# Unread TensorE products between the steps of a causal attention, and layer weights loaded later

## What is computed

```python
qkv = einsum('bsi,oi->bso', x, w_qkv) + b_qkv       # x: 2 x 1024 x 128
q, k = rope(q), rope(k)
scores = einsum('bhqd,bhkd->bhqk', q, k) / sqrt(8)
scores = where(causal, scores, lowest)
ex = exp(scores - max(scores))
attn = ex / (sum(ex) + 1e-8)
out = einsum('bhqk,bhkd->bhqd', attn, v) @ w_out.T + b_out
```

## Time and profile before

| | us |
|---|---|
| median of three runs | 2311.33 (2304.25 to 2318.38) |
| the profiled execution | 2307.12 |
| its span, first to last instruction | 2305.3 |
| TensorE busy | 2014.6 (87%) |
| VectorE busy | 1809.4 (78%) |
| ScalarE busy | 1665.7 (72%) |
| GpSimd busy | 1267.5 (55%) |
| mean granted TensorE clock | 0.941 |

### The profile page before, as it was taken

One profiled execution on the slowest core, in us unless ns is written; L12 is line 12 of the kernel. 1 busy time (PEld: TensorE's weight loads), 2 busy tenths in 40 slices (PEclk: granted clock), 3 DMA queues, 4 the chain that ended last, 5 costly groups with the idle time before them and its releaser, 6 DMA issues. The chain is left out here.

```text
span 2305.3 us, 55541 instructions
## 1 busy us (share of the span) xinstructions
PE 2014.6 (87%) x20349; PEld 1353.3 (59%) x20349; DVE 1809.4 (78%) x3609; ACT 1665.7 (72%) x3163; POOL 1267.5 (55%) x1132
## 2 busy tenths in 40 slices
PE   5788888579999999999999999999999999984283
PEld 3233332346766776776767677677767776673152
DVE  4666660699999999999999999999999999834623
ACT  2265555378888888888898888888888888864123
POOL 4400000477777677767777776776677677711052
PEclk8799997699999999999999999999999999996587
DMA  6321100211111121111211111101211111100511
GB/s 160 97 58 26 23 2 2 66 36 38 29 38 29 30 86 29 38 29 38 77 38 29 39 57 49 38 29 38 77 38 29 33 35 32 35 20 26 186 35 66
DMA packets 70562, 107.36 MB, mean 47 GB/s; under 512 B 20887, under 2 KB 47774, under 8 KB 68734
## 3 DMA queue, kind: packets, MB, share of 16 engines
q1 hardware_dynamic: 68262, 100.87, 15.2%
q0 software_dynamic: 1280, 2.62, 0.4%
q10 hardware_dynamic: 752, 0.33, 0.1%
HBM read 41.60 MB, written 12.26 MB: 23 GB/s over the span
## 5 line engine op out<-in xcount | busy, mean ns | idle before, releaser
L1446 POOL TENSOR_TENSOR qk<-rot_cos,rot_sin 128x512 f32<-128x512 f32 x256 | 323.2, 1274 | 160.3 <-DVE rot_sin L1247 160.3
L1245 DVE TENSOR_TENSOR rot_cos<-pA,layer_tab 128x512 f32<-128x512 f32 x384 | 262.8, 684 | 65.6 <-ACT sq L1086 58.7
L1456 POOL TENSOR_TENSOR qk<-qk,rnorm 128x512 f32<-128x512 f32 x256 | 262.9, 1043 | 88.0 <-DVE rnorm L1280 88.0
L382 ACT ACTIVATE probs_by_key<-pT 128x512 f32<-128x512 f32 (+3 forms) x384 | 176.9, 489 | 155.2 <-PE pT L298 119.8
L1086 ACT ACTIVATE sq<-pA 128x512 f32<-128x512 f32 x384 | 228.4, 595 | 55.9 <-PE pA L873 46.1
L439 DVE TENSOR_REDUCE minus_max<-pS 128x1 f32<-128x1024 f32 (+7 forms) x256 | 184.3, 753 | 106.4 <-PE pS L270 105.8
L1257 DVE TENSOR_REDUCE sumsq<-sq 128x8 f32<-128x512 f32 x384 | 253.4, 670 | 14.8 <-ACT sq L1086 14.6
L1247 DVE TENSOR_TENSOR rot_sin<-pA,layer_tab 128x512 f32<-128x512 f32 x384 | 260.8, 679 | 0.0
L1146 ACT ACTIVATE probsT<-pD 64x512 f32<-64x512 f32 x384 | 226.4, 589 | 43.8 <-PE pD L914 40.3
L1463 POOL TENSOR_TENSOR probs<-probs,row_inverse 128x1024 f32<-128x1024 f32 x96 | 182.7, 1904 | 104.9 <-DVE row_inverse L1316 104.9
L1106 ACT ACTIVATE qT<-pC 64x512 f32<-64x512 f32 x384 | 225.9, 588 | 7.3 <-PE pC L888 0.5
(11 more groups left out here) (313 smaller groups left out, 4619.4 us busy)
## 6 DMA issues: line engine op xcount, KB each, us to landing
v_shifted<-v SPq DMA_DIRECT2D x96, 384.0 KB, 3.5
v_shifted<-v SPq DMA_DIRECT2D x95, 128.0 KB, 3.4
q_stack<-stacked SPq DMA_DIRECT2D x24, 192.0 KB
k_stack<-stacked SPq DMA_DIRECT2D x24, 192.0 KB
W_ahead<-in_Wqkv_dram SPq DMA_DIRECT2D x12, 384.0 KB
layer_weights<-in_Wqkv_dram SPq DMA_DIRECT2D x12, 384.0 KB
stacked<-part SPq DMA_DIRECT2D x32, 128.0 KB, 2.4
tokens_in<-tokens SPq DMA_DIRECT2D x2, 1024.0 KB
```

The lines of the kernel that those rows point to most:

```text
L1245: dve.tensor_tensor(t1[c % 2][:, :].rearrange("p (h g d) -> p h g d", g=2, d=32), a, tabl[s % 2][:, j].unsqueeze(1).broadcast_to([P, 8, 2, ...
L1446: pool.tensor_tensor(qk(s, c), t1[c % 2][:, :], t2[c % 2][:, :], ALU.add).then_inc(added[c], 1)
L1456: pool.tensor_tensor(v, v, rn[p % 2][:, o:o + 8].unsqueeze(2).broadcast_to([P, 8, DH]), ALU.mult).then_inc(scaled[c], 1)
```

## The change

A helper `filler(out, n)` issues `n` bf16 products of the identity with the 256 columns of `cm` into a PSUM region that nobody reads. They stand: 60 before the first row block; 2 behind each of the row blocks 14 to 42; 2 behind the blocks at u = 1 and 3 of every later group and 3 behind `turn_maxima` there; 1 behind each of the last 66 pieces. The first two kinds write `OT[1]` and bring two waits for kept jobs; the others write the second bank of the `S` tensor whose first bank holds a narrow block or the maxima. And the load of the first window layer's weights and of the two tables moves in SP's queue from ahead of the loop over groups to behind the stacks of group 7 (g = 4).

```diff
@@ -203,15 +203,16 @@
                 load_stacks(g)
             sp.wait_ge(w_turned, 2)
             sp.dma_start(wr[:, 0, :], w["a_b_out"].rearrange("(a n) -> a n", a=1).broadcast_to([P, D])).then_inc(bo_in, 16)
-            load_layer(sp, w, env["W0"], 0, env["w0_loaded"])
-            sp.dma_start(env["xpos"][:], w["xpos"]).then_inc(env["const_loaded"], 16)
-            sp.dma_start(env["mask"][:], w["mask"]).then_inc(env["const_loaded"], 16)
             for g in range(GROUPS):
                 load_maxima(g)
                 if g < 2:
                     late_stores(2 + g)
                 if g >= 1 and g - 1 + SLOTS_G < GROUPS:
                     load_stacks(g - 1 + SLOTS_G)
+                if g == 4:
+                    load_layer(sp, w, env["W0"], 0, env["w0_loaded"])
+                    sp.dma_start(env["xpos"][:], w["xpos"]).then_inc(env["const_loaded"], 16)
+                    sp.dma_start(env["mask"][:], w["mask"]).then_inc(env["const_loaded"], 16)
 
         @block.tensor
         def _(pe):
@@ -257,6 +258,14 @@
             pe.wait_ge(mask_in, 16)
             pe.wait_ge(ident_cast, 1)
 
+            def filler(out, n):
+
+                for _ in range(n):
+                    pe.matmul(out, identb[:, :], cm[:, :, :], start=True, stop=True, skip_group_check=True)
+
+            def half_of(at):
+                return S[at % 2][:, 512:512 + 2 * P]
+
             def row_block(g, u):
                 h, qt = u // TB, TURNS[u % TB]
                 at, r = rows_at(g, u), g % SLOTS_G
@@ -315,18 +324,29 @@
             done = 0
             for j in range(EARLY_JOBS):
                 job(j)
+            pe.wait_ge(job_kept, 4)
+            filler(OT[1][:, 0:2 * P], 60)
             for it in range(GROUPS + 2):
                 if it == GROUPS:
                     turn_maxima(GROUPS - 1)
                 for u in range(NS):
                     if it < GROUPS:
                         row_block(it, u)
+                        if 14 <= NS * it + u < LEAD - 1:
+                            if NS * it + u == 14:
+                                pe.wait_ge(job_kept, 12)
+                            filler(OT[1][:, 0:2 * P], 2)
                     if it == 0 and u % 2 == 0 and EARLY_JOBS + u // 2 < NJ:
                         job(EARLY_JOBS + u // 2)
+                    if 1 <= it < GROUPS and u in (1, 3):
+                        filler(half_of(rows_at(it, u)), 2)
                     if 1 <= it < GROUPS and u == MAX_AT:
                         turn_maxima(it - 1)
+                        filler(half_of(maxima_at(it - 1)), 3)
                     for n in range(done, chunks_by(it, u)):
                         chunk(n)
+                        if it >= GROUPS and not (it == GROUPS + 1 and u >= OUT_AT):
+                            filler(half_of(maxima_at(GROUPS - 1)), 1)
                         if n % GH == 1 and n > GH:
                             values((n - GH - 1) // GH)
                     done = chunks_by(it, u)
```

## The result

| | before | changed |
|---|---|---|
| median, us | 2311.9 | 2301.9 |
| profiled execution, us | 2307.1 | 2303.3 |
| its span, us | 2305.3 | 2301.5 |
| mean granted clock | 0.941 | 0.952 |

The ratio of changed to before is 0.9956 (95% interval 0.9938 to 0.9975, 11 executions): faster by 0.44%, some 10 us, a little less than the 13.2 of the forecast and within its range. The executions of before spread from 2304 to 2320 us, those of the changed kernel from 2294 to 2305.

The account below looks back on a forecast made before the run. TensorE at half clock in three places of the causal attention (first 402 us) was taken as the bound; 0.75 + 5.0 + 0 + 7.5 + 0 = 13.2 us off the 2311.3 median gave 2298, range 2293 to 2303.

Parts of the forecast that it names:

- The stretch and the price: Causal attention, to near 402 us, half clock in three places; a filler product 0.107 us at full clock, 0.213 at half.
- Before the first block: 60 products before the first score block: 0.75 us gained, ends -2.8 and +1.5, the block not delayed.
- Early blocks: Pairs behind blocks 14 to 42: 1.4 + 0.75 + 2.8 = 5.0 us gained, ends -1.5 and +6.3.
- The third term: From 89.97 us, where TensorE also has pieces and paces: clock back at full before 90, 2.8 us gained.
- Group changes: Seven products per later change: exposed last pairs cost 1.3 us, an avoided dip gains 1.3; net 0.
- The tail: Products behind the last 66 pieces: clock holds, gross 10.0 us less 2.5 cost, net 7.5 gained, next stage included.
- Rival 1: Only the tail holds, early clock at half until the pieces start: gain 7 us, 2304; chance 0.24.
- 3: The tail falls all the same and its fillers cost time; early 5.0 us won, 2312; chance 0.09.
- 4: Slower: fillers in pacing stretch and tail all exposed, first block late; 2328 if early part wins nothing; chance 0.05.
- 5: The clock doesn't count unread products as work, so they only cost: 2317; chance 0.06.
- Rival 2: Clock full from 42 to 402 us but for moments, fillers hidden: gain 19 us, 2292; chance 0.11.
- six signs of being right: First block punctual; eight maxima blocks 7 us; clock full at 90; copies 38.2 to 38.6; four tail rounds 10.6; next stage full.

Follow-up runs that it names:

- e3: The change with 100 instead of 60 products ahead of the first score block; median 2296.1 us, ratio to before 0.9934.
- e8: e6 without the pair behind the block at u = 3 of every group; median 2293.1 us, ratio to before 0.9905, four executions.
- e1: The change with only the tail's 66 products left, weights still loaded later; median 2303.5 us, ratio to before 0.9984 (0.9952 to 1.0017).
- e5: The change without any unread products, only the later load of weights and tables; median 2317.1 us, ratio to before 1.0015.
- e7: e3 without the products at the changes of groups; median 2305.6 us, ratio to before 0.9956.
- e11: e8 plus 8 products ahead of the last output's transposes and 16 behind them; median 2292.0 us, ratio to before 0.9912.
- e2: The change without the 66 products behind the last pieces; median 2301.5 us, ratio to before 0.9955.
- e10: e6 without the tail's products; median 2302.3 us, ratio to before 0.9956.
- e4: The change with weights and tables loaded at their old place, ahead of the loop over groups; median 2299.2 us, ratio to before 0.9937.
- e6: e3 with 4 products behind each of blocks 14 to 43 and 34 at the first group change; median 2293.3 us, ratio to before 0.9913.

## Why the prediction held, and where it didn't

**The stretch and the price.** Right. A product costs some 0.11 us (60 in 6.7, 100 in 11.1), where 0.107 was forecast. Every gain that the profiles show lies where the clock is full in place of half, in the causal stage and the stage behind it. One reading was off: the 6 in the row of 40 slices is the eighth, from 403 us on, behind the causal attention.

**Before the first block: the first step that failed.** The forecast took 0.75 us of a possible 1.5. The products ended at 37.8 us, near the 38.4 that was worked out, 4.3 us ahead of the block, and the clock fell at 41.2, just before it; then it was at half until 48.1 us, where in before it was full again at 46.0, and the term came out as -0.8. What stood there as a sentence apart, that idleness between bursts brings the half clock back (the Trainium skill, "TensorE: Matmul & The Clock Gate", section "HAM oscillation — how this bites in real kernels"), was the better guide. The trace agrees: full at 38 us, half at 42, with TensorE idle between. That the clock had survived 3.8 us of idleness in before was taken as a chance, and was read too long: in before it became full only at 32.4 us, behind the last job, and fell at 35.8. Where the products reach up to the block, in e3, the clock stays full.

**Early blocks: the step that missed most.** Right in two of three terms. From the ninth block to the split of the maxima 1.5 us were won (forecast 1.4). Over the twelve blocks from the second group's first maximum 0.75 were won, as forecast, with the fall at the change of groups that was foreseen: 13.19 us in before (77.03 to 90.22), 12.44 in the change (76.08 to 88.52), all of it in the last four blocks. The line of VectorE in before:

```profile
90.22 1.52 DVE L439 TENSOR_REDUCE minus_max<-pS 128x1 f32<-128x768 f32 x2 [0.69 <-PE pS L270]
```

The third term, 2.8 us for pieces at full clock, failed: 0.3 us were won from there to the first scores behind the value products, and 0.2 lost again up to the value copy. The clock, back at 82, fell again at 89, where the pairs end (block 42) and the engine waits 0.8 us before block 42 and again before block 44, and came back only at 96. Whether the end of the pairs did it isn't shown: e3 has the same products there, and its clock stayed full. The value copy won 2.6 us over the whole stretch, 0.3 of it at the split, not 5.0. "Back at full before 90" was right and not enough: it had to last.

**Group changes.** The net of 0 was right (0.2), and the exposed pair, 0.21 us a group, was named and measured at 0.22, with the other five at nothing (e8). That the net came out so was luck: it rests on one dip in the one profile of before. What the products insure against was mis-sized: that dip cost 1.3 us; of the five other falls at later changes, in e1, e5 and e7, two cost 1.2 each and three 7.6, 7.6 and 2.9. One profile held one draw of something that varies, and the sum took it for the value.

**The tail.** Forecast 7.5 with the next stage, measured 8.0. The price was 0.27 us for four rounds of pieces (10.52 against 10.25), 1.1 in all where 2.5 were taken; the next stage gave 0.75 of 1.3, since the clock fell again at its start (392.8 us; where it is full at the right time, as in e11, that stage takes 15.7 us, 1.1 less). That the clock would hold was right, in all eight profiles. But 8.0 is the difference of two profiles. What was missing is that a tail without products doesn't always fall (e2): over all executions the tail's products alone gave 0.16% (e1, not clear of nothing), the change without them the whole 0.45% (e2), and behind a dense early stretch they gave 9 us (e10 against e8). The term has no single value.

**The weights.** Worth nothing, as forecast (e4, e5); their transfers ended before the maxima store was due.

**The rivals.** Rival 1 came nearest in the early part, since the clock wasn't held there until the pieces, and its 2304 is nearer to the measured 2301.9 than the 2298 of the forecast, so that the number alone can't choose between the two; 3, 4 and 5 are out: the tail held, the pieces lost 0.07 us a round, and unread products do count. Rival 2, clock full from 42 to 402, is what e6 and e8 built, with 20 to 22 us against the before measured beside them (0.9913 and 0.9905), near the 19 that it gave. Of the six signs of being right two didn't come: the clock was 0.50 at 90 us, and the clock was at half from 392.8 to 396.2 us, while the next stage's first products ran.

**What is left open.** Why TensorE, busy without a gap, stayed at half clock for 24 us in e5 and in e7 and came back after some 3 us in the dip of before and in e2, wasn't tested. Nor was what it is in the unread products that holds the clock, the idle time that they fill or their shape (all 128 rows, where scores use 72 and pieces 75): no run put in others. Why e2 times as well as the change, though e10 shows what a tail without products can cost, is open too. And the exact shares of the places can't be told: medians of the same kernel before differed by up to 8 us between comparisons (2308.3 beside e1, 2316.6 beside e5).

## What to carry to other kernels

Where TensorE waits for others in a short regular pattern, its clock can fall to half and stay there, at random from one execution to the next; here, unread products in places where it waits anyway cost nothing to be seen and took the loss and, with 100 ahead of the first block (e3, e6, e8, e11), most of the spread away. Put them up to the very instruction that is waited for (60 that ended 4 us too early brought nothing), and not ahead of one that others wait for. Before pricing such a loss from one profile, look at the spread of the times and mean clocks over executions: the profile shows one draw.

## What the runs showed of the hardware

- A full queue doesn't bring the clock back by itself: 24 us at half with TensorE busy all the time (e5, 313.4 to 337.3 us, and e7, 153.5 to 177.4 us), of bf16 products with 72 and 75 of 128 rows and float32 value products.
- With the engine idle the full clock lasted about 3.4 us behind the 60 products (37.8 to 41.2). In before it ended 3.8 us after the last job, and had become full only 0.4 us after it (32.4 to 35.8).
- The mean granted clock of an execution orders its time within one kernel: in before 0.944 goes with 2302 to 2307 us, 0.937 with 2315 to 2318, 0.927 to 0.929 with 2328 to 2330.
